# Two-layer transformer: attention scores moved to F32R row strips, keys split by GpSimd, queries kept on chip, maxima sent by DMA

## What is computed

```
scores = einsum('bqhd,khd->bhqk', Q, K) * 0.25
attn   = softmax(scores, axis=-1)
out    = einsum('bhqk,khd->bqhd', attn, V)
```

## Time and profile before

| | |
|---|---|
| runs | 2119.72, 2120.23, 2126.68 us; median 2120.23 |
| profiled execution | 2117.09 us, its span 2115.3 us |
| layer 0 attention | about 112 to 885 us of the span |
| layer 1 attention block | about 1035 to 1285 us |
| mean granted TensorE clock | 0.925 of full |
| PE, DVE, ACT, POOL busy | 85%, 66%, 54%, 14% |

### The profile page before, as it was taken

How to read it: one execution, slowest core, us unless ns; L and a number is a source line. 1 busy time by engine, 2 the same in 40 slices (tenths; PEclk the granted TensorE clock), 3 DMA queues, 4 the chain that set the end, 5 groups by cost and what they waited for, 6 DMA issues and landing times. The chain is left out here.

```text
span 2115.3 us, 31356 instructions
## 1 busy us (share of the span) xinstructions
PE 1808.1 (85%) x9772; PEld 970.4 (46%) x9772; DVE 1399.7 (66%) x1846; ACT 1147.7 (54%) x2253; POOL 285.7 (14%) x447
## 2 busy tenths in 40 slices
PE   4499999999999999645699973499999999949997
PEld 3122222222222233133222221388888888748886
DVE  6487777877777888246467753666666666656665
ACT  3067767776777777513377762255445454424432
POOL 3210000000000000102111111211111111002223
PEclk8599999999999999856799986799999999979999
DMA  7201111111111200112312222100000000023432
GB/s 284 96 34 35 40 46 35 41 39 36 35 39 35 89 16 16 36 56 55 112 65 70 72 101 73 39 14 20 7 20 20 20 12 10 1 51 115 121 105 65
DMA packets 56274, 115.00 MB, mean 54 GB/s; under 512 B 7249, under 2 KB 21585, under 8 KB 54123
## 3 DMA queue, kind: packets, MB, share of 16 engines
q1 hardware_dynamic: 53715, 109.21, 15.9%
q10 hardware_dynamic: 2456, 4.46, 0.8%
HBM read 83.52 MB, written 30.12 MB: 54 GB/s over the span
## 5 line engine op out<-in xcount | busy, mean ns | idle before, releaser
L348 DVE TENSOR_REDUCE a_max_part<-psum 128x1 f32<-128x1024 f32 x640 | 759.6, 1220 | 253.8 <-PE psum L265 253.8
L389 ACT ACTIVATE a_probs<-psum 128x512 f32<-128x512 f32 x1280 | 675.1, 603 | 247.9 <-PE psum L309 242.7
L265 PE MATMUL psum<-a_k_rows,a_q_rows 96*128 96x512 bf16 x1280 | 399.6, 395 | 52.0 <-DMA a_q_rows<-q_parts 26.1
L309 PE MATMUL psum<-a_q_rows,a_k_rows 99*128 99x512 bf16 x1280 | 410.3, 386 | 29.6 <-ACT a_probs L389 29.3
L300 PE MATMUL psum<-a_probs,a_v_ext 128*32 128x512 f32 x2560 | 342.5, 607 | 6.1 <-ACT a_o_out L373 3.8
L265 PEld LDWEIGHTS psum<-a_k_rows,a_q_rows 96*128 96x128 bf16 x1280 | 98.8, 98 | 407.0 <-issue 193.0
L309 PEld LDWEIGHTS psum<-a_q_rows,a_k_rows 99*128 99x128 bf16 x1280 | 124.1, 98 | 268.8 <-ACT a_probs L389 155.4
L1548 PE MATMUL psum<-high_t_parts,high_gu 128*128 128x512 f32 x600 | 145.6, 393 | 6.8 <-DVE high_t_parts L1642 6.8
L1253 PE MATMUL psum<-wide_k_t,wide_q_t 128*128 128x512 f32 (+3 forms) x576 | 130.3, 353 | 1.7 <-DVE wide_id_bf L1452 1.7
L1548 PEld LDWEIGHTS psum<-high_t_parts,high_gu 128*128 128x128 f32 x600 | 113.6, 190 | 31.3 <-issue 7.3
L226 POOL TENSOR_TENSOR a_max_bf<-a_neg_max,a_zeros 128x4 bf16<-128x4 f32 x64 | 13.2, 206 | 849.0 <-DVE a_neg_max L352 849.0
(11 more groups left out here) (173 smaller groups left out, 1871.1 us busy)
## 6 DMA issues: line engine op xcount, KB each, us to landing
o<-a_o_out SPq DMA_DIRECT2D x64, 256.0 KB, 2.1
gu_in<-in_w_gu SPq DMA_DIRECT2D x25, 256.0 KB, 3.0
k_parts<-keys_parts SPq DMA_DIRECT2D x12, 512.0 KB, 6.5
a_k_rows<-k_parts SPq DMA_DIRECT2D x16, 384.0 KB
high_cw<-cw SPq DMA_DIRECT2D x24, 256.0 KB, 3.9
setup_k_in<-in_k SPq DMA_DIRECT2D x4, 1024.0 KB, 15.2
a_k_rows<-k_parts SPq DMA_DIRECT2D x16, 256.0 KB
a_v_in<-in_v SPq DMA_DIRECT2D x16, 256.0 KB, 14.8
```

The costliest lines, as they stand in the source:

```text
L265: mm = pe.matmul(psum[:, 2 * (n % 2) + j, :], q_rows[0:KROWS, b, q0:q0 + P], k_rows[0:KROWS, b, k0:k0 + 512], start=True, stop=True)
L309: pe.matmul(psum[:, bank_of(filling(j)), :], k_rows[0:SROWS, b, j * P:(j + 1) * P], q_rows[0:SROWS, b, half * QH:(half + 1) * QH], start=T ...
L348: dve.tensor_reduce(max_part[:, u % 2, c // nch, c % nch:c % nch + 1], psum[:, 2 * (n % 2):2 * (n % 2) + 2, :], AX.XY, ALU.max).then_inc(s ...
L389: act.activation(probs[:, j % pring, :], psum[:, bank_of(filling(j)), :], ACT.Exp).then_inc(exp_done, 1)
```

## The change

- **Rows.** Queries and keys are each split in two F32R parts (high and low) and three products of 16 rows make 48 rows (q high x k high, q low x k high, q high x k low), with the three rows of maxima at 48 to 50. These are laid out twice, in partitions 0 to 50 and 64 to 114 (a strip each): the strips hold the first and the second half of the keys, and neighbouring matmuls use different strips and different banks. `shift` goes from 3 to 6 (first pass further ahead), the maxima are turned 6 chunks before the end of a u, not 2.
- **Keys.** They are loaded whole (F32, from the input or from `k1`) into one buffer `k_in`; GpSimd makes both parts per head (`split_keys`: one pass over 128 partitions, two over 16), the first head in `setup`'s block (`prefetch`). SyncE loads a head's keys when GpSimd has split those of the head before.
- **Queries.** `project` leaves both parts in SBUF in layer 0, and SyncE copies 16 partitions at a time into `q_rows`; in layer 1 they go through DRAM (`q1`).
- **Maxima.** ScalarE writes the three rows to `max_row`; SyncE sends them to both strips with two DMAs (`send_maxima`), and the first second-pass matmul of the u waits for their landing.
- **Sums.** VectorE copies them out of PSUM, not ScalarE. All loops are written out. Sums of 15 heads (before: 12) are loaded back in one go before the last u's (`load_sums`).

```diff
-KROWS = NPROD * HD
-MROW = 96
-SROWS = MROW + 3
-PRODUCTS = [(0, 0, 0, 3), (48, 0, 1, 2), (80, 0, 2, 1)]
+STRIP = 64
+MROWS = 3
+LOW_K, MROW = 32, 48
+SROWS = MROW + MROWS
...
-        def load_k(eng, h, b):
-            for row, kp, qp, n in PRODUCTS:
-                eng.dma_start(k_rows[row:row + n * HD, b, :], k_parts[kp:kp + n, h, :, :]).then_inc(kq_loaded[b], 16)
-        def load_q(eng, h, b):
-            for row, kp, qp, n in PRODUCTS:
-                eng.dma_start(q_rows[row:row + n * HD, b, :],
-                              q_parts[qp:qp + 1, h, :, :].broadcast_to([n, HD, T])).then_inc(kq_loaded[b], 16)
+    def strip_of(self, j, rows):
+        return slice(STRIP * (j % 2), STRIP * (j % 2) + rows)
+    def load_k(self, sp, h):
+        keys = self.k_dram[HD * h:HD * h + HD, :]
+        for n in range(2):
+            part = keys[:, n * self.per_strip:(n + 1) * self.per_strip]
+            at = STRIP * n
+            sp.dma_start(self.k_in[at:at + 2 * HD, :],
+                         part.unsqueeze(0).broadcast_to([2, HD, self.per_strip])).then_inc(self.k_loaded, 16)
+            sp.dma_start(self.k_in[at + LOW_K:at + MROW, :], part).then_inc(self.k_loaded, 16)
+    def split_keys(self, pool, h):
+        b = h % self.nb
+        pool.wait_ge(self.k_loaded, 64 * (h + 1))
+        pool.tensor_tensor(self.k_rows[:, b, :], self.k_in[:, :], self.zeros[:, 0:1].broadcast_to([P, self.per_strip]),
+                           ALU.add).then_inc(self.k_high, 1)
+        pool.wait_ge(self.k_high, h + 1)
+        for s in range(2):
+            low = slice(STRIP * s + LOW_K, STRIP * s + MROW)
+            pool.tensor_tensor(self.k_rows[low, b, :], self.k_in[low, :], self.k_rows[low, b, :],
+                               ALU.subtract).then_inc(self.k_split, 1)
+        pool.wait_ge(self.k_split, 2 * h + 2)
...
+        def heads_split(u):
+            return min(H, self.early + u + 1, nb + u // 2)
+            def send_maxima(u):
+                b, half = (u // 2) % nb, u % 2
+                sp.wait_ge(self.row_ready, u + 1)
+                for s in range(2):
+                    sp.dma_start(q_rows[STRIP * s + MROW:STRIP * s + SROWS, b, half * QH:(half + 1) * QH].bitcast(F32),
+                                 self.max_row[0:MROWS, u % 2, :]).then_inc(self.rows_loaded[u % 2], 16)
...
+            sent = self.early + 1
+            send_maxima(0)
+            for u in range(us):
+                h, half = u // 2, u % 2
+                if u + 1 < us:
+                    send_maxima(u + 1)
+                sp.wait_ge(self.o_full, u + 1)
+                sp.dma_start(self.o_dram[h, :, half * QH:(half + 1) * QH], self.o_out[:, half, :]).then_inc(self.o_stored[half], 16)
+                if half == 1 and h + nb < H:
+                    load_q(sp, q_rows[:, h % nb, :], h + nb, self.q_loaded[h % nb])
+                while sent < min(H, heads_split(u) + 1):
+                    sp.wait_ge(self.k_split, 2 * sent)
+                    self.load_k(sp, sent)
+                    sp.wait_ge(self.v_ready, sent)
+                    self.load_v(sp, sent)
+                    sent += 1
+                if u == us - 3:
+                    for n in range(2):
+                        sp.wait_ge(self.o_stored[n], 16 * (H - 1))
+                    load_sums(sp, o4, self.o_dram, 0, H - 1, self.o4_loaded)
...
+            def slot(u, g):
+                j = group * g
+                one = u * steps + 2 * g + ahead
+                two = one + 1
+                second_wait(u, j)
+                second_wait(u, j + 1)
+                second_chunk(u, j)
+                second_chunk(u, j + 1)
+                if one < self.chunks:
+                    first_wait(one)
+                    first_half(one, 0)
+                    first_half(one, 1).then_inc(self.s1_full, 1)
+                if j + 2 == self.turn_at and u + 1 < us:
+                    turn_maxima(u + 1)
+                second_wait(u, j + 2)
+                second_chunk(u, j + 2)
+                if two < self.chunks:
+                    first_wait(two)
+                    first_half(two, 1)
+                    first_half(two, 0).then_inc(self.s1_full, 1)
+                second_wait(u, j + 3)
+                second_chunk(u, j + 3)
+                if g > 0:
+                    pv_group(u, g - 1)
+                elif u > 0:
+                    pv_group(u - 1, groups - 1)
-            def position(it, p, last):
-                u, j = p // nkt, p % nkt
-                if j % 2 == 0:
-                    for numbered in first_pass(last)[1]:
-                        step, shifted = numbered[1][0], p // 2
-                        if step == shifted or step + bu * steps == shifted:
-                            first_pass_chunk(it + (step != shifted), numbered)
-                if j == turn_at and not (last and u == bu - 1):
-                    turn_maxima(it, u + 1)
-                second_chunk(it, u, j)
-                if j % group == group - 1:
-                    if j >= 2 * group - 1:
-                        pv_group(it, u, j // group - 1)
-                    elif u > 0:
-                        pv_group(it, u - 1, groups - 1)
...
+            def take_sums(u):
+                half = u % 2
+                dve.wait_ge(self.pv_done, (u + 1) * groups)
+                if u >= 2:
+                    dve.wait_ge(self.o_stored[half], 16 * (u // 2))
+                dve.tensor_copy(self.o_out[:, half, :], psum[:, 7, :]).then_inc(self.o_full, 1)
-            def take_sums(it, u):
-                half = u % 2
-                act.wait_ge(pv_done, it * (bu * groups) + (u + 1) * groups)
-                act.wait_ge(o_stored[half], it * (16 * nb) + 16 * (u // 2 + 1))
-                act.activation(o_out[:, half, :], psum[:, 7, :], ACT.Copy).then_inc(o_full, 1)
```

More of the change, by code:

```diff
@@ new lines, in _ @@
+            pool.wait_ge(self.v_const, 2)
+            self.copy_v(pool, 0)
+            for h in range(1, self.early):
+                self.split_keys(pool, h)
+                self.copy_v(pool, h)
+            done = self.early
+            split_max(0)
+            for u in range(us):
+                if u + 1 < us:
+                    split_max(u + 1)
+                for h in range(done, heads_split(u)):
+                    self.copy_v(pool, h)
+                    self.split_keys(pool, h)
+                done = heads_split(u)
@@ L269, in bank_free, with first_half @@
-            def bank_free(it, u, n):
-                if n < ring:
+                    pe.wait_ge(self.s1_free, n - 1)
+                if c == 0 and u % 2 == 0:
+                    h = u // 2
+                    pe.wait_ge(self.q_loaded[h % nb], 16 * q_loads * (h // nb + 1))
+                    pe.wait_ge(self.k_split, 2 * h + 2)
+            def first_half(n, s):
+                u, c = n // steps, n % steps
+                b, half, qt, ch = (u // 2) % nb, u % 2, c // self.nch, c % self.nch
+                q0, k0 = half * QH + qt * P, ch * 512
+                rows = self.strip_of(s, MROW)
+                return pe.matmul(psum[:, 2 * (n % 2) + s, :], q_rows[rows, b, q0:q0 + P], k_rows[rows, b, k0:k0 + 512],
+                                 start=True, stop=True)
@@ L330, in _ @@
[L330 to L341 removed]
+                mm.then_inc(self.pv_done, 1)
@@ new lines, in _ @@
+            put_row(0)
+            for u in range(us):
+                for j in range(nkt):
+                    p = u * nkt + j
+                    if j == self.turn_at and u + 1 < us:
+                        put_row(u + 1)
+                    act.wait_ge(self.s2_full, p + 1)
+                    if p >= self.pring and p % group == 0:
+                        act.wait_ge(self.pv_done, (p - self.pring) // group + 1)
+                    act.activation(self.probs[:, p % self.pring, :], psum[:, self.bank_of(self.filling(j)), :],
+                                   ACT.Exp).then_inc(self.exp_done, 1)
@@ new lines, in project, with _ @@
+        if q_out is not None:
+            @block.sync
+            def _(sp):
+                heads = P // HD
+                for c in range(DC):
+                    sp.wait_ge(high_done, 2 * c + 2)
+                    sp.wait_ge(low_done, 2 * c + 2)
+                    for at, src in ((0, q_high), (HD, q_low), (2 * HD, q_high)):
+                        sp.dma_start(q_out[heads * c:heads * (c + 1), at:at + HD, :], src[:, c, :].bitcast(F32)).then_inc(stored, 16)
+                for c in range(DC):
+                    sp.wait_ge(k_taken, 2 * c + 2)
+                    sp.dma_start(k_out[c * P:(c + 1) * P, :], k_sb[:, c, :]).then_inc(stored, 16)
@@ L1721, in adaln_two_layers, with load_q @@
                       loads=[(wqkv[:, :, :, :].rearrange("p c i n -> p c (i n)"), chunks(i["wqkv1"]))])
[L1722 removed]
+            q_high = part.enter_context(nc.sbuf_tensor("q_high1", [P, DC, T], F32R))
+            q_low = part.enter_context(nc.sbuf_tensor("q_low1", [P, DC, T], F32R))
```

(10 more changed lines are left out.)

556 lines of the change are left out of this document (224 added, 332 removed).

## The result

The changed kernel takes 2267.68 us, the median of four runs (2262.82 to 2280.21); the kernel before 2120.32 (2119.72 to 2126.68). The ratio is 1.069, 95% interval 1.065 to 1.073: slower by 147 us. The profiled execution is the longest of the four, 2280.21 us with a span of 2278.0, 162.7 more than the span before; times of stages are from it, so they add up to more than 147.

The account below looks back on a forecast made before the run. TensorE was taken as the bound. From 2117.1 us, layer 0 gave -77, layer 1 +94 and the clock +15, making 2149; the median of runs lies 3 us higher: 2152 us, range 2065 to 2205.

Parts of the forecast that it names:

- the ring of layer 1: Layer 1: send, landing, scores, sums, copy and store follow one another each half head; 7.0 us bare, mean 9.2 with loads.
- the price of a late send: Layer 0: next maxima landing at the edge behind key loads, some 0.5 us for 13 heads; 6 us (0 to 40).
- the bare half head: Layer 0: eight groups of 2.57 us and a turning group 0.5 longer; 21.2 us (19.6 to 24.1).
- the sign: Layer 1: TensorE's idle time before second scores put down to the DMA of the maxima row, more than 100 us.
- an early half head of layer 1: Layer 1's first half heads, with key loads and split in the ring: 13.5 us, 14.5 with queries; six of 14.2.
- the front of layer 0: Layer 0: about 49 us from attention block start to first second score, at 110.5, 2 us earlier than before.
- Both signs of "worse than the range": A clock fall inside layer 0, or first-pass waits for `k_split`, would make the time worse than 2205 us.
- The rival without overlap: Layer 0: score matmuls in two strips don't overlap, a half head stays at 24 us; 2232 us, chance 0.12.
- a faster whole: Layer 1's ring is short, below 7.5 us a half head on average; 2083 us, or 2032 at best; chance 0.25.
- Key loads, layer 0: Layer 0: loads of the next head's keys hold up what is queued behind them for 10 us (2.1 to 19.5).
- The clock: Layer 1: TensorE idles in each half head and partly runs at the lower clock; 15 us (0 to 50).
- The sends: Layer 1: sending the maxima takes 0.46 us to issue and 2.0 to land in each half head.

Follow-up runs that it names:

- experiment 2: Changed kernel with each head's keys loaded by six DMAs of 16 partitions, not two double-reading broadcasts and two plain ones: 2190.91 us, ratio 1.031.
- experiment 11: Changed kernel plus maxima sent ahead, fewer heads split early in layer 1, loads ahead of sends; key loads keep the two-fold reads: 2098.51 us, ratio 0.990.
- experiment 1: Changed kernel with the maxima of half head u+2 sent before the sums of u are stored: 2143.04 us, ratio 1.008.
- experiment 4: Changed kernel with 16 repeats of first-pass matmuls on TensorE ahead of each wait for maxima in layer 1: 2269.73 us.
- experiment 10: Changed kernel plus maxima sent ahead, one copy a DMA, and keys and values issued ahead of the next maxima: 2071.30 us, ratio 0.978.

## Why the prediction was wrong

The direction and the ring of layer 1 were right, the size was not: 2152 us forecast (2065 to 2205), 2267.7 measured. The step that failed is the price of a late send: in layer 0 the prediction put the maxima behind the key loads at 6 us (40 at most) and kept the lower clock out of that layer; they cost 55, half of it at the lower clock. The strips overlap, layer 0's group takes 2.61 us (2.57 forecast), the bare half head 21.3 (21.2), the idle time before second scores is put down to the DMA of the maxima (63 us in layer 1, where the sign asked for more than 100; 54 more are called "issue"), and layer 1's stores are 9 to 18 us apart while there are loads. Two sums are slightly off: the terms of an early half head of layer 1 add up to 13.8, not 13.5, those of the front of layer 0 to 48 at most, not 49. Both signs of "worse than the range" came true: the clock fell inside layer 0, and at the head of layer 1 the first pass waited 30 us for the split of the keys (`k_split`). The rival without overlap is refuted, and so is a faster whole. The terms that were mis-sized:

| term | forecast | measured |
|---|---|---|
| layer 0: first second score | 110.5 | 118.9 |
| layer 0: maxima late behind key loads | 6 (0 to 40) | 27 waiting + 28 at the lower clock |
| layer 0: `load_sums` | 11 | 19 |
| layer 0 in all | -77 | -2 |
| layer 1: block start to first store | 30.5 | 41.8 |
| next 7 half heads | 93 | 112.5 |
| 13 with loads | 120 | 144.7 |
| 9 bare | 63 | 68.1 |
| last two and `load_sums` | 38 | 46.7 |
| layer 1 in all | +94, and +15 for the clock | +161.5 |

In layer 0 the 19 are 31.4 + 30.3 - 2 x 21.3, from the last two stores, and the 55 of the middle are 819.99 - 146.83 - 29 x 21.3. The measured terms leave some 7 us unnamed. They lie in the first half head: its store comes 146.8 - 118.9 = 27.9 us after its first second score, at a mean granted clock of 0.81.

- **Key loads, layer 0** ("I take 10 us" for how long they hold the queue). The send, issued 10 us behind the first load, landed 15.7 us behind it (386.61 to 402.3), where TensorE had no time left: 2.1 us a head waited where 0.5 stood. The range of the hold, up to 19.5 us, had this; its price, 40 us at most, had not, for want of the clock. Experiments 2 and 11 show the cause of the hold: with one copy a DMA there is no such wait, with the two-fold reads there is. (The estimate set beside it by the Trainium skill's page "DMA: Bandwidth & Descriptors", 9 us for the two broadcasts, was no warning either.)
- **The clock.** The prediction kept it to layer 1 and to 15 us (0 to 50), and said that a fall inside layer 0 would make it worse than the range. It fell in both. In layer 0 a wait of 2 us was paid twice (experiment 1). In layer 1, first score to sums took 2.81 us and the sums 1.93 in most half heads with loads, 2.07 and 1.06 in bare ones: some 1.5 us each, 19 over the 13. That share is read from durations and experiment 4 bears it out in part. For the seven before, where TensorE's turning waits in between, it isn't taken apart.
- **The sends.** I counted the issue of one, 0.46, ahead of a landing of 2.0. Two are issued, 1.41, and the second has to land: 1.9 in the ring shown, 2.2 in the mean of those with loads, 1.28 in bare ones. So issue and landing are 3.3 to 3.6 us with loads instead of 2.46, and 2.65 without. That a bare half head took the forecast 7.0 us is luck: sends 0.9 dearer, landing 0.7 and the way from the sums to the end of the copy 0.4 cheaper.
- **Ends.** `load_sums` and both starts were too cheap by 8 to 11 us each. The start of layer 0 hangs on the key loads as well: with one copy a DMA its first second score stands at 100.2, 10 us earlier than forecast.

## What to carry to other kernels

Put what the next stage waits for at the head of its queue: a send of 6 KB stood behind a store and loads that nobody waited for yet, and moving it ahead was worth some 125 us. What counts is who waits: with the sends two half heads ahead, it paid to put the loads ahead of them again (experiment 10, some 40 us), since GpSimd waited for those. When a wait is priced, price the matmuls behind it too: here each wait of 2 us on TensorE cost 4. And a work item that several engines hand on (load, copy, split, turn, send) is priced by its ring, and in layer 1 it was cured by starting its parts earlier, not by making its steps faster. In layer 0 a faster load was a cure as well (experiment 2), and a needed one once the loads stood ahead of the sends (experiment 11). With loads and sends in order and one copy a DMA the same F32R layout takes 2016 us instead of 2268, 5% less than the kernel before.

## What I had not expected of the hardware

- The lower clock outlasts the wait. In windows of 10 us behind five waits of 1.6 to 3.0 us the granted clock was 0.82, 0.57, 0.82, 0.65 and 0.51, though TensorE was busy for all but 0.05 us of each; the lowest stands behind the shortest wait. What sets its length is open.
- In `setup`, VectorE's operations on 1024 elements took 5.51 and 4.87 us beside GpSimd's split of the keys; the first of them took 1.22 before. The block ended at 43.1 us, only 0.6 earlier than before. The slow operations can account for 2.5 us of that at most, for GpSimd's own work in the block lasts until 40.6:
```profile
30.35 10.26 POOL L164 TENSOR_TENSOR a_k_rows<-a_k_in,a_k_rows 16x2048 fp32r<-16x2048 f32 x2
30.74 5.51 DVE L538 SCALAR_TENSOR_TENSOR setup_size<-mod_row 128x1024 f32<-128x1024 f32 x1
36.29 4.87 DVE L540 TENSOR_SCALAR setup_sign<-setup_sign 128x1024 f32<-128x1024 f32 x1
```
```profile
39.85 1.22 DVE L510 SCALAR_TENSOR_TENSOR setup_size<-mod_row 128x1024 f32<-128x1024 f32 x1
```
The page "SBUF — State Buffer" of the Trainium skill (section "SBUF: two separate sides") says that a VectorE operation with two SBUF inputs, or in a mode that uses two ports, and one of GpSimd take a shared pair of ports in turn, for a whole instruction. The trace agrees: GpSimd's two instructions, merged in the first row, end at 35.17 and 40.62, and the two VectorE operations 1.1 and 0.5 us behind them.
- In layer 0 GpSimd took 4.57 us for 16 x 2048 elements and 3.60 for 128 x 2048 (there the second operand is one column): fewer partitions did not make it cheaper.
